# The order of score tiles and everything else inside a step of a three-unit attention pipeline

## Chip, cores and metric

One NeuronCore of a Trainium2 chip runs the kernel. The metric is the device time of one execution in microseconds (us), lower is better; the time before is the median of 3 runs.

## What is computed

The program embeds tokens, mixes them with one low-rank attention layer, routes each of 16 sequences to an expert, runs three 8-head attentions for each sequence, and ends with a feed-forward layer. The change is in the three attentions. In the reference they are (cut):

```
def _spatial_experts(xn, idx, in_w, in_b, out_w, out_b):      # "S", 512 x 512, 8 heads of 16
    att = softmax(einsum('bthd,bshd->bhts', q, k), axis=-1)
    o = einsum('bhts,bshd->bthd', att, v).reshape(B, T, D)
...
def _temporal_experts(...):                                    # "T", causal
    logits = where(causal, einsum('bthd,bshd->bhts', q, k) * HD ** (-0.5), -inf)
...
def _cross_mha(q_in, kv_in, ...):                              # "C", q from S's output, k and v from T's
...
fused = _cross_mha(spatial_out, temporal_out, ...)
```

## The kernel before, in words

`attend` works on 48 units: S, T and C of each of 16 sequences. A unit has 32 score tiles (8 heads by 4 blocks of 128 rows). Each unit goes through four stages, and a software pipeline has four units at work at once. Time is cut into slots of 32 steps (`TILES`). In a slot TensorE (called PE in the rows) works for:

- unit `kn`, the next: three projections to q, k and v, at steps 3, 9 and 12 to 15 (`PROJECT_AT`, L1200 and L1204)
- unit `ka`: one score tile a step (`score`, L1217, 128 rows by the keys). VectorE (DVE) reduces each tile to the row maxima, negated (`reduce`, L1022; for T with the causal mask, L1018)
- unit `kb`: one logit tile a step from step 8 on (`LAG`), transposed, with the maxima folded in as further rows of the contraction (`logits`, L1237). ScalarE (ACT) turns each into exponentials (L1122). From step 17 on every fourth step has a weighted sum (`weigh`, L1256, four matmuls side by side)
- unit `ko`, the oldest: its last 8 logit tiles at steps 0 to 7, its last weighted sums at steps 1, 5, 9 and 13, and its output matmul at steps 29 and 30 (`output`, L1273 and L1276)

The slots go round in three kinds, named here by the unit that is scored: an S slot, a T slot, a C slot. The middle of the program is a hardware loop over such triples. In a T slot the score tiles of the four row blocks have 128, 256, 384 and 512 keys in turn; the tile number modulo 4 tells the width. In an S or C slot all score tiles are 512 wide.

The maxima of a unit are turned (transposed, L1226) in two halves by `turn_maxima`: the first half at step 19 of the slot in which the unit is scored, the second at step 6 of the next slot. VectorE copies each turned half out (`ng`, L1032) after its reductions 18 and 5. VectorE also keeps the values `va` (L1043) after reduction 16, swaps the sums (`s_right`, L1059) after reduction 21 (`SWAP_AT`), and takes the output of `ko` (L1082 or L1089) after reduction 31. ScalarE makes the reciprocal `s_recip` (L1149) from the swapped sums at `RECIP_AT`, by which GpSimd (POOL) scales `oT`.

Two rings of three PSUM banks couple the engines: score tile n waits until VectorE has reduced tile n-3, and logit tile n until ScalarE has read tile n-3. One further bank, the desk, is shared by projections, turned maxima and outputs, strictly one after the other (`desk_free`, `desk_full`): so the turn at step 19 waits until `va` is kept, and the k projection at step 9 waits until the second half of the maxima (`ng`) is copied out. Each engine works strictly in the order in which `slot_program` writes its instructions; no scheduler moves them.

Of the kernel before, what the change touches and what calls it, by code (L numbers as in the profile page):

```python
# [37 lines left out]
WEIGH_AFTER = 9  # L38
VALUES_AT = 16
GROUP_1_AT, GROUP_2_AT = (30, 31), (14, 15)  # L40
SWAP_AT, RECIP_AT = 21, 23
OUTPUT_AT, KEEP_AT = 29, 31
PROJECT_PARTS, OUTPUT_PARTS = (1, 1, 4), 2
LAG = 8
# [20 lines left out]
def exists(b):  # L65
    return not isinstance(b, int) or 0 <= b < B
# [14 lines left out]
def desk_use(name, b):  # L81

    if name[0] in "qkv" and name[1] == "S" and isinstance(b, int) and b == 0:
        return "qkv".index(name[0])
    i = b - DESK_BATCH[name]
    order = [u for s in DESK for u in s]
    at = order.index(name)
    if isinstance(i, int):
        return desk_count(i) + sum(exists(i + DESK_BATCH[u]) for u in order[:at])
    return DESK_FIRST + DESK_USES * (i - STEADY[0]) + at  # L90


def unit_no(kind, b):

    if kind == "C":
        return 3 * B - 1 if isinstance(b, int) and b == B - 1 else 3 * b + 4
    if isinstance(b, int) and b == 0:
        return "ST".index(kind)
    return 3 * b - 1 + "ST".index(kind)


def ring_place(kind, b, n, ring):

    steady = {"S": -1, "T": 0, "C": 4}
    u = unit_no(kind, b) if isinstance(b, int) else steady[kind] % 3
    assert 3 * TILES % ring == 0
    return (TILES * u + n) % ring


def group_place(kind, b, q):  # L110

    return ring_place(kind, b, 4 * q, 4 * RP) // 4


def at_least(eng, sem, value):

    if not isinstance(value, int) or value > 0:
        eng.wait_ge(sem, value)
# [524 lines left out]
def attend(nc, shared, s_in, s_out, t_in, t_out, c_in, c_out, c_bias):  # L643
# [3 lines left out]
    with ExitStack() as ctx:  # L647
# [90 lines left out]
        def units(i, slot):  # L738

            return ((("T", i), ("S", i), ("C", i - 2), ("T", i - 1)),  # L740
                    (("C", i - 1), ("T", i), ("S", i), ("C", i - 2)),
                    (("S", i + 1), ("C", i - 1), ("T", i), ("S", i)))[slot]
# [19 lines left out]
        def first_key(kind, tile):  # L762

            return P * (tile // 4 % NB) if kind == "T" else 0
# [41 lines left out]
        with nc.Block() as block:  # L806
# [370 lines left out]
            def _(pe):  # L1177

                def project(kind, b, c, part):

                    if not exists(b):
                        return
                    source = {"S": xn, "T": xt, "C": t_outT if c else oT_S}[kind]
                    weight = w_fold if kind == "C" and c == 0 else w_in[kind]
                    use = desk_use("qkv"[c] + kind, b)
                    if part == 0:
                        at_least(pe, desk_free, use)
                        if kind == "C":
                            if c == 0:
                                pe.wait_ge(fold_in, 16 * b + 16)  # L1190
                                pe.wait_ge(o_ready, unit_no("S", b) + 1)
                            else:
                                pe.wait_ge(desk_free, desk_use("oT", b) + 1)
                        elif c == 0:
                            pe.wait_ge(win_in[kind], 16 * b + 16)
                            pe.wait_ge(affine_done, input_no({"S": "xn", "T": "xt"}[kind], b) + 1)
                    width = T // PROJECT_PARTS[c]
                    at = slice(width * part, width * part + width)
                    if c < 2:
                        last = nc.tensor.matmul(desk[:, at], weight[:, P * c:P * c + P], source[:, at],  # L1200
                                                start=True, stop=True)
                    else:
                        for n in range(width // P * part, width // P * (part + 1)):
                            last = nc.tensor.matmul(desk[:, P * n:P * n + P], source[:, P * n:P * n + P],  # L1204
                                                    w_in[kind][:, W_V:W_V + P], start=True, stop=True)
                    if part == PROJECT_PARTS[c] - 1:
                        last.then_inc(desk_full, 1)

                def score(kind, b, n):

                    u = unit_no(kind, b)
                    if n == 0:
                        pe.wait_ge(stack_in[kind], 16 * 2 * NPROD * (b + 1))
                    at_least(pe, reduced, TILES * u + n - RL + 1)
                    hd, tb = n // NB, n % NB
                    keys = P * (tb + 1) if kind == "T" else T
                    nc.tensor.matmul(psum[:, ring_place(kind, b, n, RL), 0:keys], qs[kind][0:RA, hd, P * tb:P * tb + P],  # L1217
                                     ks[kind][0:RA, hd, 0:keys], start=True, stop=True).then_inc(scored, 1)

                def turn_maxima(kind, b, half):  # L1220

                    if not exists(b):
                        return
                    pe.wait_ge(reduced, TILES * unit_no(kind, b) + HALF * (half + 1))
                    at_least(pe, desk_free, desk_use("hm"[half] + kind, b))
                    nc.tensor.transpose(desk[0:HALF, 0:P], mx[kind][:, HALF * half:HALF * half + HALF], ident[:])\  # L1226
                        .then_inc(desk_full, 1)
# [12 lines left out]
                def weigh(kind, b, q):  # L1240

                    u = unit_no(kind, b)
                    g, s = q // NB, q % NB
                    if kind == "T":
                        pe.wait_ge(cut, 2 * NB * b + q + 1)
                    else:
                        pe.wait_ge(exped, TILES * u + 4 * q + 4)
                    if q == 0:
                        pe.wait_ge(v_ready[kind], b + 1)
                        pe.wait_ge(desk_free, desk_use("v" + kind, b) + 1)  # L1250
                        at_least(pe, high_out, u)
                    if q == NB:
                        pe.wait_ge(low_out, u + 1)
                    t0 = first_key(kind, 4 * q)
                    for j in range(4):
                        last = nc.tensor.matmul(sums[32 * j:32 * j + 32, t0:T], va[kind][:, s, g, j, :],  # L1256
                                                probs[:, group_place(kind, b, q), j, t0:T], start=(s == 0),
                                                stop=(kind == "T" or s == NB - 1), skip_group_check=(kind == "T"))
                    last.then_inc(summed, 1)
# [21 lines left out]
                def slot_program(i, slot):  # L1281
                    (kn, bn), (ka, ba), (kb, bb), (ko, bo) = units(i, slot)
                    for n in range(TILES):
                        if exists(ba):
                            score(ka, ba, n)
                        if n == TURN_AT[0]:
                            turn_maxima(ka, ba, 0)
                        if n == TURN_AT[1]:
                            turn_maxima(kb, bb, 1)
                        for c in range(3):  # L1290
                            if 0 <= n - PROJECT_AT[c] < PROJECT_PARTS[c]:
                                project(kn, bn, c, n - PROJECT_AT[c])
                        if n < LAG and exists(bo):
                            logits(ko, bo, TILES - LAG + n)
                        if n >= LAG and exists(bb):
                            logits(kb, bb, n - LAG)
                        q, rest = divmod(n - LAG - WEIGH_AFTER, 4)
                        if rest == 0 and q < 0 and exists(bo):
                            weigh(ko, bo, q + 8)
                        if rest == 0 and q >= 0 and exists(bb):  # L1300
                            weigh(kb, bb, q)
                        if 0 <= n - OUTPUT_AT < OUTPUT_PARTS and exists(bo) and ko != "S":
                            output(ko, bo, n - OUTPUT_AT)

# [13 lines left out]
                last.then_inc(folded, 1)  # L1318
                pe.wait_ge(fold_kept, 2)
                whole_loop(pe, slot_program)  # L1320


# [246 lines left out]
```

## Time and profile before

| | before |
|---|---|
| median of 3 runs | 1693.22 us (1692.04 to 1693.26) |
| the profiled execution, its own time | 1697.35 us |
| its span in the trace | 1695.5 us |
| granted TensorE clock, mean | 0.938 of full speed; 1.00 in the slots shown |
| TensorE busy (matmul records) | 1521.0 us, 90% |
| VectorE busy | 1242.6 us, 73% |
| ScalarE busy | 1102.5 us, 65% |
| GpSimd busy | 1018.9 us, 60% |

All times of the trace are counted from the start of the span. A matmul's record lasts longer than the array is occupied by it, because matmuls overlap, so for TensorE the distance between the starts of two matmuls tells more than busy time. In the windows shown below the columns are the stretch and its length in us, then the busy us (and number of instructions) of PE, PEld (TensorE's weight loads), DVE, ACT and POOL, the granted clock as a share of 2.4 GHz, the DMA engines' share and GB/s. In the timelines they are the start in us, the duration in us, engine, line, operation, written<-read, shapes, and in brackets the idle time before the instruction with what ended it.

The share of busy time is a mean over the whole program; what follows reads single slots.

### The profile page before, as it was taken

The page shows a single profiled execution, that of the slowest core. Times are in us where ns is not written, and L with a number is a line of the kernel's source. Part 1 is how long each engine was busy: PE and PEld are TensorE (multiplying, and loading weights), DVE is VectorE, ACT ScalarE, POOL GpSimd, SP SyncE. Part 2 cuts the span into 40 slices and gives each one's busy share as a digit, 9 for nine tenths or more (in the row PEclk, how much of TensorE's full clock was granted, in tenths as well). Part 3 has the DMA queues.
Part 4 walks back from the last instruction along what each step waited for, and adds up shares of the span by engine and source line. Part 5 has one row for each costly group of instructions (what it writes and reads, how often), then busy time and mean ns, then how long its engine had stood idle before and what let it go on. Part 6 is the DMA issues. An engine that isn't in the chain of part 4 may idle for free. (4 is left out here: it accounts for less than half of the span.)

```text
span 1695.5 us, 37358 instructions
## 1 busy us (share of the span) xinstructions
PE 1521.0 (90%) x8662; PEld 660.5 (39%) x8662; DVE 1242.6 (73%) x3454; ACT 1102.5 (65%) x2137; POOL 1018.9 (60%) x1375
## 2 busy tenths in 40 slices
PE   2767975889999999999999999999999999875998
PEld 0215962233333333333333333333333333212665
DVE  4995866478787878878787887878788887353442
ACT  1432770647878777787877878787777878823333
POOL 6841435466685677767567677757767775423443
PEclk9767986879999999999999999999999999957999
DMA  1321117365454565456456546546645643020221
GB/s 41 77 54 31 45 32 108 50 81 72 70 83 67 70 75 84 62 74 81 61 75 77 77 60 83 75 60 81 77 72 65 85 63 55 10 30 29 62 67 56
DMA packets 134645, 109.27 MB, mean 64 GB/s; under 512 B 24128, under 2 KB 127552, under 8 KB 134592
## 3 DMA queue, kind: packets, MB, share of 16 engines
q1 hardware_dynamic: 132544, 104.45, 41.9%
q0 software_dynamic: 2048, 4.20, 1.0%
q8 instruction: 23, 0.38, 0.1%
q14 instruction: 30, 0.25, 0.1%
HBM read 19.26 MB, written 8.39 MB: 16 GB/s over the span
## 5 line engine op out<-in xcount | busy, mean ns | idle before, releaser
L1122 ACT ACTIVATE probs<-psum 128x512 f32<-128x512 f32 (+3 forms) x1536 | 757.9, 550 | 256.2 <-PE psum L1237 247.4
L1022 DVE TENSOR_REDUCE mx_S<-psum 128x1 f32<-128x512 f32 x512 | 324.7, 679 | 50.3 <-PE psum L1217 50.0
L1022 DVE TENSOR_REDUCE mx_C<-psum 128x1 f32<-128x512 f32 x512 | 316.3, 676 | 32.0 <-PE psum L1217 32.0
L1018 DVE CUSTOM_DVE_ANT_0 psum<-psum,causal 128x128 f32<-128x128 f32 (+3 forms) x512 | 241.4, 515 | 95.3 <-PE psum L1217 94.2
L1217 PE MATMUL psum<-ks_S,qs_S 96*128 96x512 bf16 x512 | 197.0, 395 | 17.9 <-DVE mx_S L1022 8.7
L1217 PE MATMUL psum<-ks_C,qs_C 96*128 96x512 bf16 x512 | 199.8, 398 | 12.2 <-DVE mx_C L1022 9.5
L1237 PE MATMUL psum<-qs_C,ks_C 99*128 99x512 bf16 x512 | 188.6, 387 | 3.3 <-ACT probs L1122 2.9
L1237 PE MATMUL psum<-qs_S,ks_S 99*128 99x512 bf16 x512 | 188.0, 384 | 0.2 <-ACT probs L1122 0.2
L903 POOL CAST parts_q<-f_q 128x512 bf16<-128x512 f32 x48 | 29.2, 609 | 251.1 <-ACT f_q L1113 250.6
L1217 PE MATMUL psum<-ks_T,qs_T 96*128 96x128 bf16 (+3 forms) x512 | 157.4, 310 | 5.1 <-DVE mx_T L1018 3.7
L1237 PE MATMUL psum<-qs_T,ks_T 99*128 99x256 bf16 (+3 forms) x512 | 152.3, 302 | 1.8 <-ACT probs L1122 1.7
L1256 PE MATMUL psum<-probs,va_C 128*32 128x512 f32 x1024 | 137.2, 608 | 0.8 <-ACT u_all L1142 0.6
L1256 PE MATMUL psum<-probs,va_S 128*32 128x512 f32 x1024 | 136.4, 604 | 1.7 <-ACT u_all L1142 0.5
L891 POOL TENSOR_SCALAR_AFFINE_SELECT probs<-probs 128x512 f32<-128x512 f32 x128 | 81.1, 634 | 57.4 <-ACT probs L1122 56.7
L1217 PEld LDWEIGHTS psum<-ks_C,qs_C 96*128 96x128 bf16 x512 | 49.9, 98 | 167.0 <-DVE mx_C L1022 121.2
L1217 PEld LDWEIGHTS psum<-ks_S,qs_S 96*128 96x128 bf16 x512 | 50.0, 98 | 154.5 <-DVE mx_S L1022 111.0
L1469 ACT ACTIVATE gT<-psum,b 128x512 f32<-128x512 f32 x64 | 44.0, 687 | 95.2 <-PE psum L1489 95.2
L1217 PEld LDWEIGHTS psum<-ks_T,qs_T 96*128 96x128 bf16 x512 | 50.6, 99 | 138.6 <-DVE mx_T L1018 95.5
L1256 PE MATMUL psum<-probs,va_T 128*32 128x512 f32 (+3 forms) x1024 | 96.0, 447 | 3.2 <-POOL probs L891 2.4
L957 POOL TENSOR_TENSOR s_all<-s_all,s_high 128x512 f32<-128x512 f32 x48 | 60.9, 1269 | 24.9 <-ACT u_high L1132 24.1
L317 POOL DMA_INDIRECT h<-in_table,ids x64 | 61.4, 960 | 21.4 <-issue 17.4
L1237 PEld LDWEIGHTS psum<-qs_C,ks_C 99*128 99x128 bf16 x512 | 49.5, 98 | 63.4 <-ACT probs L1122 27.5
(182 smaller groups left out, 2720.1 us busy)
## 6 DMA issues: line engine op xcount, KB each, us to landing
qs_S<-parts_q SPq DMA_DIRECT2D x96, 128.0 KB, 4.4
ks_S<-parts_k SPq DMA_DIRECT2D x96, 128.0 KB, 4.8
qs_T<-parts_q SPq DMA_DIRECT2D x96, 128.0 KB, 4.5
ks_T<-parts_k SPq DMA_DIRECT2D x96, 128.0 KB, 4.6
qs_C<-parts_q SPq DMA_DIRECT2D x96, 128.0 KB, 4.4
ks_C<-parts_k SPq DMA_DIRECT2D x96, 128.0 KB, 4.8
w_in_S<-in_s_in SPq DMA_DIRECT2D x16, 257.0 KB, 2.8
w_in_T<-in_t_in SPq DMA_DIRECT2D x16, 257.0 KB, 2.7
```

What stands on the lines that cost most here:

```text
L317: nc.gpsimd.indirect_dma_start(h[:, NB * b + n, :], None, table, bass.IndirectOffsetOnAxis(ap=ids[:, NB * b + n:NB * b + n + 1].bitcast(U3 ...
L891: nc.gpsimd.affine_select(out=diagonal, in_=diagonal, compare_op=ALU.is_ge, fill=0.0, base=0, pattern=[[0, 4], [1, P]], channel_multiplier ...
L903: nc.gpsimd.tensor_copy(parts[c][:, 0, :], f32[c][:]).then_inc(hi_done, 1)
L957: nc.gpsimd.tensor_tensor(s_all[:], s_all[:], s_high[:], ALU.add).then_inc(s_merged, 1)
L1018: nc.vector.tensor_tensor_reduce(tile[:, 0:last_key], tile[:, 0:last_key], causal[:, T - last_key:T], 1.0, NEG, ALU.add, ALU.max, mx[kind] ...
L1022: nc.vector.tensor_reduce(mx[kind][:, n:n + 1], tile, AX_X, ALU.max, negate=True).then_inc(reduced, 1)
L1122: nc.scalar.activation(probs[:, group_place(kind, b, n // 4), n % 4, t0:T], psum[:, LOGITS + ring_place(kind, b, n, RC), t0:T], ACT.Exp, s ...
L1217: nc.tensor.matmul(psum[:, ring_place(kind, b, n, RL), 0:keys], qs[kind][0:RA, hd, P * tb:P * tb + P], ks[kind][0:RA, hd, 0:keys], start=T ...
L1237: nc.tensor.matmul(psum[:, bank, t0:T], ks[kind][0:RB, hd, P * s:P * s + P], qs[kind][0:RB, hd, t0:T], start=True, stop=True).then_inc(log ...
L1256: last = nc.tensor.matmul(sums[32 * j:32 * j + 32, t0:T], va[kind][:, s, g, j, :], probs[:, group_place(kind, b, q), j, t0:T], start=(s == 0),
L1469: nc.scalar.activation(gT[:, odd, f, :], psum[:, 1 + f, :], ACT.Gelu, bias=b1[:, f:f + 1])\
```

## The change

In TensorE's `slot_program` the score tile of a step is written after the turns, projections, logit tile and weighted sums of that step, where it was written before them. The output matmul stays behind the score tile. On ScalarE the reciprocal moves from step 23 to step 24, one exponential later. VectorE's, GpSimd's and the DMA queue's programs are the same; no instruction is added or removed.

```
-SWAP_AT, RECIP_AT = 21, 23
+SWAP_AT, RECIP_AT = 21, 24
...
                 def slot_program(i, slot):
                     (kn, bn), (ka, ba), (kb, bb), (ko, bo) = units(i, slot)
                     for n in range(TILES):
-                        if exists(ba):
-                            score(ka, ba, n)
                         if n == TURN_AT[0]:
                             turn_maxima(ka, ba, 0)
...
                         if rest == 0 and q >= 0 and exists(bb):
                             weigh(kb, bb, q)
+                        if exists(ba):
+                            score(ka, ba, n)
                         if 0 <= n - OUTPUT_AT < OUTPUT_PARTS and exists(bo) and ko != "S":
                             output(ko, bo, n - OUTPUT_AT)
```

On TensorE, in the first T slot that also has projections (written out ahead of the loop), from step 3 to step 9, before the change:

```order
L1217 MATMUL psum<-ks_T,qs_T 128x512
L1200 MATMUL psum<-oT_S,w_fold 128x512
L1217 MATMUL psum<-ks_T,qs_T 128x128
L1217 MATMUL psum<-ks_T,qs_T 128x256
L1217 MATMUL psum<-ks_T,qs_T 128x384
L1226 MATMUL psum<-ident,mx_S 16x128
L1217 MATMUL psum<-ks_T,qs_T 128x512
L1217 MATMUL psum<-ks_T,qs_T 128x128
L1237 MATMUL psum<-qs_S,ks_S 128x512
L1217 MATMUL psum<-ks_T,qs_T 128x256
L1200 MATMUL psum<-t_outT,w_in_C 128x512
```

The same stretch after it:

```order
L1217 MATMUL psum<-ks_T,qs_T 128x384
L1200 MATMUL psum<-oT_S,w_fold 128x512
L1217 MATMUL psum<-ks_T,qs_T 128x512
L1217 MATMUL psum<-ks_T,qs_T 128x128
L1217 MATMUL psum<-ks_T,qs_T 128x256
L1226 MATMUL psum<-ident,mx_S 16x128
L1217 MATMUL psum<-ks_T,qs_T 128x384
L1217 MATMUL psum<-ks_T,qs_T 128x512
L1237 MATMUL psum<-qs_S,ks_S 128x512
L1217 MATMUL psum<-ks_T,qs_T 128x128
L1200 MATMUL psum<-t_outT,w_in_C 128x512
```

The kinds of matmul follow each other as before; in every place of a score tile stands the tile before it (384 keys where 512 stood, and so on). The turn of `mx_S` now follows tile 5 and not tile 6.

On TensorE, around the turn at step 19 of the same slot, before the change:

```order
L1256 MATMUL psum<-probs,va_S 32x512 x4
L1217 MATMUL psum<-ks_T,qs_T 128x384
L1237 MATMUL psum<-qs_S,ks_S 128x512
L1217 MATMUL psum<-ks_T,qs_T 128x512
L1226 MATMUL psum<-ident,mx_T 16x128
L1237 MATMUL psum<-qs_S,ks_S 128x512
```

And after it:

```order
L1256 MATMUL psum<-probs,va_S 32x512 x4
L1217 MATMUL psum<-ks_T,qs_T 128x256
L1237 MATMUL psum<-qs_S,ks_S 128x512
L1217 MATMUL psum<-ks_T,qs_T 128x384
L1226 MATMUL psum<-ident,mx_T 16x128
L1237 MATMUL psum<-qs_S,ks_S 128x512
```

The turn of the first half of T's maxima keeps its place among TensorE's instructions and stands behind tile 18 where it stood behind tile 19.

On ScalarE, in the second slot with a reciprocal, as one piece of the difference:

```order
 L1122 ACTIVATE probs<-psum 128x384
 L1122 ACTIVATE probs<-psum 128x256 x4
-L1122 ACTIVATE probs<-psum 128x128 x3
-L1149 ACTIVATE s_recip<-s_right 128x512
-L1122 ACTIVATE probs<-psum 128x128
+L1122 ACTIVATE probs<-psum 128x128 x4
+L1149 ACTIVATE s_recip<-s_right 128x512
 L1122 ACTIVATE probs<-psum 128x512 x4
```

One more exponential of 128 columns now stands ahead of the reciprocal.

## Rows read from the trace of the kernel before

**Rows 1.** The page's busy time by engine.

```profile
PE 1521.0 (90%) x8662; PEld 660.5 (39%) x8662; DVE 1242.6 (73%) x3454; ACT 1102.5 (65%) x2137; POOL 1018.9 (60%) x1375
```

**Rows 2.** Windows: an S, a T and a C slot (from VectorE's first reduction to the next).

```profile
711.43:736.88 25.45, 25.08 (x155) 9.72 (x154) 22.51 (x42) 19.78 (x41) 17.71 (x25) 1.00 0.54 81
736.88:762.08 25.20, 24.88 (x154) 9.72 (x150) 17.93 (x74) 21.26 (x41) 16.67 (x22) 1.00 0.55 69
762.08:786.25 24.17, 23.26 (x142) 8.73 (x134) 21.19 (x40) 17.66 (x39) 17.94 (x26) 1.00 0.55 71
```

**Rows 3.** Waits of the whole span: us in total, times, longest.

```profile
DVE ng L1032 <- PE psum L1226: 41.1, 48, 4.5
```

**Rows 4.** Timeline, TensorE, S slot, steps 6, 8 and 9.

```profile
715.41 0.39 PE L1217 MATMUL psum<-ks_S,qs_S 96*128 96x512 bf16 x1
...
716.31 0.38 PE L1237 MATMUL psum<-qs_C,ks_C 99*128 99x512 bf16 x1
717.02 0.39 PE L1217 MATMUL psum<-ks_S,qs_S 96*128 96x512 bf16 x1 [0.33 <-DVE mx_S L1022]
717.24 1.02 PE L1200 MATMUL psum<-xt,w_in_T 128*128 128x512 f32 x2
```

**Rows 5.** Timeline, VectorE, the same stretch.

```profile
716.08 0.28 DVE L1032 TENSOR_SCALAR ng<-psum 16x128 f32<-16x128 f32 x1 [0.39 <-PE psum L1226]
716.29 2.46 DVE L1022 TENSOR_REDUCE mx_S<-psum 128x1 f32<-128x512 f32 x4
```

**Rows 6.** Timeline, T slot: VectorE's copy, and TensorE at steps 8 and 9.

```profile
741.32 0.28 DVE L1032 TENSOR_SCALAR ng<-psum 16x128 f32<-16x128 f32 x1 [1.07 <-PE psum L1226]
...
741.71 0.38 PE L1237 MATMUL psum<-qs_S,ks_S 99*128 99x512 bf16 x1
742.29 0.28 PE L1217 MATMUL psum<-ks_T,qs_T 96*128 96x256 bf16 x1 [0.20 <-DVE mx_T L1018]
```

**Rows 7.** Timeline, TensorE, C slot, steps 8 and 9.

```profile
767.61 0.38 PE L1237 MATMUL psum<-qs_T,ks_T 99*128 99x512 bf16 x1
767.97 0.39 PE L1217 MATMUL psum<-ks_C,qs_C 96*128 96x512 bf16 x1
```

**Rows 8.** Timeline, S slot: swap on VectorE; TensorE's score tiles 22, 25 and 26.

```profile
728.05 0.70 DVE L1059 STREAM_SHUFFLE s_right<-s_all 128x512 f32<-128x512 f32 x1
...
727.88 0.39 PE L1217 MATMUL psum<-ks_S,qs_S 96*128 96x512 bf16 x1
...
728.99 0.38 PE L1237 MATMUL psum<-qs_C,ks_C 99*128 99x512 bf16 x1
729.41 0.39 PE L1217 MATMUL psum<-ks_S,qs_S 96*128 96x512 bf16 x1
...
730.94 0.39 PE L1217 MATMUL psum<-ks_S,qs_S 96*128 96x512 bf16 x1
```

**Rows 9.** Timeline, TensorE, T slot, steps 24 to 25 and 28 to 29.

```profile
754.43 0.38 PE L1237 MATMUL psum<-qs_S,ks_S 99*128 99x512 bf16 x1
754.85 0.28 PE L1217 MATMUL psum<-ks_T,qs_T 96*128 96x256 bf16 x1
...
757.16 0.38 PE L1237 MATMUL psum<-qs_S,ks_S 99*128 99x512 bf16 x1
757.48 0.28 PE L1217 MATMUL psum<-ks_T,qs_T 96*128 96x256 bf16 x1
```

**Rows 10.** Timeline, S slot: values kept on VectorE, and the turn at step 19.

```profile
723.99 0.75 DVE L1043 TENSOR_TENSOR va_T<-psum,w_in_T 128x256 f32<-128x256 f32 x2
...
725.59 0.27 PE L1226 MATMUL psum<-ident,mx_S 128*16 128x128 f32 x1
```

**Rows 11.** Timeline, C slot: its second half on VectorE, ScalarE and TensorE.

```profile
780.28 6.04 DVE L1022 TENSOR_REDUCE mx_C<-psum 128x1 f32<-128x512 f32 x10
...
780.49 0.63 ACT L1149 ACTIVATE s_recip<-s_right 128x512 f32<-128x512 f32 x1 [0.78 <-DVE s_right L1059]
...
781.00 0.39 PE L1217 MATMUL psum<-ks_C,qs_C 96*128 96x512 bf16 x1 [0.62 <-DVE mx_C L1022]
```

More of the change, by code:

```diff
@@ L40 @@
 GROUP_1_AT, GROUP_2_AT = (30, 31), (14, 15)
-SWAP_AT, RECIP_AT = 21, 23
+SWAP_AT, RECIP_AT = 21, 24
 OUTPUT_AT, KEEP_AT = 29, 31
@@ L1283, in slot_program @@
                     for n in range(TILES):
-                        if exists(ba):
-                            score(ka, ba, n)
                         if n == TURN_AT[0]:
@@ L1301, in slot_program @@
                             weigh(kb, bb, q)
+                        if exists(ba):
+                            score(ka, ba, n)
                         if 0 <= n - OUTPUT_AT < OUTPUT_PARTS and exists(bo) and ko != "S":
```

## The prediction

> **What bounds the kernel now.** I read the page first. TensorE has the most busy time, then VectorE, ScalarE and GpSimd [rows 1]. But matmul records overlap, so this settles nothing. The windows come next, cut at VectorE's first reduction of each slot: an S, a T and a C slot take 25.45, 25.20 and 24.17 us, together 74.8 us at full clock, and VectorE is busy for 22.5, 17.9 and 21.2 us of them [rows 2]. The hardware loop runs 13 such triples (`STEADY`), and partly filled ones stand ahead of it and behind it.
>
> What decides is the distance between the starts of TensorE's matmuls. A matmul with 512 columns is followed 0.22 us later by the next one where nothing is late (717.02 to 717.24) [rows 4]. Where a distance is larger, TensorE stood still for the difference. Laid over a whole triple, TensorE streams almost without a break in the S and T slots and in the first half of a C slot, and stands still at few places:
>
> - S slot, score tile 9: it comes 0.71 us after the logit tile before it (716.31 to 717.02), so 0.49 us are lost [rows 4].
> - T slot, tile 9: 0.58 us, 0.36 lost [rows 6]. C slot, tile 9: 0.36 us, 0.14 lost [rows 7].
> - S slot, tile 25: 0.42 us, 0.20 lost [rows 8]. T slot, tile 25: 0.42, 0.20 lost; tile 29: 0.32, 0.10 lost [rows 9].
> - second half of the C slot: here VectorE is the bound. It does ten reductions in 6.04 us without a gap, one each 0.60 us, and tile 25 waits for it (idle 0.62 us by the record's modelled end) [rows 11].
>
> Two causes stand behind the first five. Tile 9 waits for reduction 6, and reduction 6 waits behind the copy `ng`, which waits for the turn at step 6. That turn stands behind score tile 6, which stands behind the weighted sum of step 5. VectorE has reduced tile 5 long before: it idles 0.39 us ahead of `ng` in the S slot [rows 5] and 1.07 us in the T slot [rows 6], 41.1 us in 48 waits in all [rows 3]. And tile 25 waits for reduction 22, which stands behind the swap (0.70 us) [rows 8].
>
> **The change part by part.** No instruction is added or removed, so all durations stay. On TensorE the sequence of kinds is the same; only the score tile in each place is the one before. I call place n what held tile n. Place n now holds tile n-1. Seen from TensorE, then, every reduction comes in the same place, and the extras of VectorE (`ng`, `va`, swap, outputs) come one reduction later. The ring of three is unchanged in these terms: place n waits for the reduction of place n-3.
>
> *The copy `ng` at step 5.* It now follows the reduction of place 6, so reduction and turn run side by side. S slot: the tile in place 6 starts at 715.41 and takes 0.39 [rows 4], so its reduction can begin at 715.84 and ends near 716.5 with the 0.67 us of one (2.46 less three spacings of 0.60) [rows 5]; before it began at 716.29. Place 9 can follow at about 716.55, when TensorE is free anyway (716.31 + 0.22 = 716.53). The 0.49 us are gone. T slot and C slot have 0.36 and 0.14 to lose and VectorE was idle longer there (1.07 us in the T slot), so these go too. Sum 0.99 us for each triple. What is late next: the k projection in place 9 waits for `ng` to free the desk. `ng` now starts after the reduction, near 716.45, and takes 0.28 us: 716.7, while TensorE reaches the projection at 716.55 + 0.22 = 716.77. The margin is under 0.1 us. If it is missed in each slot by as much as 0.1 us, 48 slots give back 4.8 us.
>
> *The swap.* It comes after the reduction of place 22, so place 25 no longer waits for it: 0.20 + 0.20 us back, and 0.10 at tile 29 of the T slot, whose reduction of place 26 is now of the 256-key tile and shorter. Sum 0.50 us for each triple. The 0.70 us of the swap used to lie under the weighted sum of step 21; now they lie behind it, so I follow them [rows 8]. The tile in place 22 starts at 727.88 and is done at 728.27, its reduction ends near 728.97, so place 25 can go at 729.2, as soon as TensorE is free (728.99 + 0.22). The swap lasts to about 729.6, the next reduction (place 23) to 730.2. Place 26 waits for that one; it comes 1.53 us after place 25 (729.41 to 730.94), now at 730.7. So the swap is hidden again, with 0.5 us to spare. Bounds: all 0.50 us back, or none; I take all.
>
> *The values `va`.* One reduction later, 0.60 us. They end at 724.74 in the S slot and the turn at step 19, which waits for them on the desk, starts at 725.59 [rows 10]: 0.85 us of cover, 0.25 left. No cost. VectorE's wait for the turn gets no longer, since the turn stands one tile earlier.
>
> *Projections, outputs and weighted sums* keep their places. The output at step 29 now stands behind the next score tile, which feeds VectorE 0.4 us earlier after the long block; VectorE is not the bound there. No gain is counted.
>
> *The reciprocal.* The swap ends one reduction later, 0.60 us, and the reciprocal one exponential later. In the C slot ScalarE already waits 0.78 us for it [rows 11] and has slack (17.7 busy of 24.2 us) [rows 2]. In the T slot ScalarE is busy for 21.3 of 25.2 us, so a longer wait could be absorbed. Counted at nothing; if the wait were 0.3 us longer in each of the 32 fuller slots and reached TensorE, it would cost 10 us, which is in the upper end of the range.
>
> *The C slot's second half* stays as long as it is, since VectorE's work there is the same.
>
> *The sum.* 0.99 + 0.50 = 1.49 us for a triple, 13 triples in the loop: 19.4 us. The partly filled triples at both ends have smaller waits of the same kind, about 1 us together. Against this, VectorE runs one tile behind TensorE, which costs 0.6 us once. 19.8 us off. The profiled execution took 1697.35 us by its own clock, 4.1 us above the median of the runs; its own would become 1677.6, and the median 1693.2 - 19.8 = 1673.4 us. I forecast 1674.
>
> **A rule of the skill against this.** Rows first: weight loads are busy for 39% of the span, VectorE for 73% [rows 1]. The Trainium skill, "Perfetto Trace Analysis", section "Identifying the Most-Contended Engine", judges TensorE's headroom by its weight loads and not by its matmul records; by it VectorE would be the engine to relieve here. What that would make of the time is the fourth rival below. The starts of the matmuls 0.22 us apart [rows 4] speak against it: the array is taken, although weight loads are not.
>
> **The rivals.**
> - *Half of it (chance 0.17).* The `ng` part works, the swap part does not: the swap's 0.70 us stop place 26 instead of place 25. Gain 0.99 x 13 = 13 us, 1680 us; with the desk missed by 0.1 us each time, 1685. For it: the swap loses its cover under a weighted sum. Against: VectorE has 3 to 7 us of idle time in the S and T slots [rows 2].
> - *The waits only move, or ScalarE hands the gain back (0.07).* 1690 to 1696 us. For it: several engines are each two thirds to nine tenths busy. Against: the places of loss are fed by VectorE alone.
> - *Slower (0.05).* The turn at step 19 catches VectorE before `va` is kept, and TensorE stands. The cover is 0.85 us, one reduction takes 0.60 of it [rows 5, 10]. Each 0.1 us that the values come later than I think, beyond 0.25 us, costs 4.8 us over 48 slots; the gain is eaten up at 0.41 us of stall a slot, and at 0.55 us the time is 1700 us.
> - *VectorE is the bound everywhere (0.04).* Then what counts is its idle time ahead of `ng`, 41.1 us [rows 3]: 1652 us. Against: in the T slot it is busy for 17.9 of 25.2 us [rows 2], and cannot be the bound there.
>
> **How the numbers follow.** My forecast's own case has 0.67, with 1670 to 1679 us. The range of 1667 to 1687 adds the half case whole and a few us below for waits in the first and last slots; it leaves out the second, third and fourth rival, 0.16, and a little of the tails. A change of 0.2%, 3.4 us, is about what can be told from none. Faster: 0.67 + 0.17 + 0.04 and a part of the second rival, 0.89; same 0.06; slower 0.05.
>
> **What would show it.** Right: the wait of `ng` for the turn falls from 41 us to under 5; in S, T and C slots tiles in place 9 and 25 follow 0.22 us after the logit tile (0.1 after a narrow one); an S slot takes about 24.8 us, a T slot 24.6, a C slot 24.0, a triple 73.3; TensorE still idles in the second half of the C slot. Wrong: a new wait on TensorE ahead of L1226 or of L1200 for the desk, a wait of L1149 above 24 us in the T and S slots that ends in late logit tiles, or a longer C slot.

## The result, and the profile after

The changed kernel takes **1672.98 us** (median of 4 runs, 1671.79 to 1673.13), against 1693.24 for the kernel before (1692.04 to 1693.40, 4 runs on the same chip). The ratio is 0.9882 (95% interval 0.9871 to 0.9894), so 20.3 us less. The forecast was 1674 us, its sum 19.8 us less.

The page's busy line and the windows of an S, a T and a C slot, cut at VectorE's first reduction as in [rows 2] (columns: PE, PEld, DVE, ACT, POOL busy, granted clock, DMA share, GB/s):

```profile
PE 1517.6 (91%) x8662; PEld 661.0 (40%) x8662; DVE 1245.2 (75%) x3454; ACT 1106.5 (66%) x2137; POOL 1020.2 (61%) x1375
```

```profile
702.17:726.91 24.74, 24.74 (x154) 9.57 (x146) 22.52 (x41) 19.71 (x40) 17.14 (x24) 1.00 0.54 76
726.91:751.40 24.49, 24.40 (x154) 9.66 (x150) 18.00 (x74) 21.19 (x40) 16.64 (x22) 1.00 0.56 71
751.40:775.59 24.19, 23.89 (x146) 9.00 (x142) 21.21 (x41) 18.08 (x40) 18.57 (x27) 1.00 0.57 76
```

No engine executes fewer instructions (the counts are those of [rows 1]). The S slot is 0.71 us shorter, the T slot 0.71, the C slot not at all (24.17 before): a triple falls from 74.82 to 73.42 us, by 1.40. I forecast 1.49. Over the 39 slots that the hardware loop accounts for (score tile 0 of the sixth slot to that of the 45th), the trace shows 971.96 us before and 954.31 now: 17.65 us. The first five slots lose 0.46 us, the last four gain 1.46 (up to their last score tile) and what follows them 1.27. These ends say little: the kernel of e2 below takes the same 971.9 us as before over the 39 slots, and differs by 1.3 us in the first five. The two spans differ by 24.4 us, and 4.5 us of that lie ahead of the first score tile, where nothing was changed; the profiled execution of before stood 4.1 us above its median.

Now the places. TensorE, S slot, steps 8 and 9, and VectorE in the same stretch:

```profile
706.52 0.38 PE L1237 MATMUL psum<-qs_C,ks_C 99*128 99x512 bf16 x1
706.80 0.39 PE L1217 MATMUL psum<-ks_S,qs_S 96*128 96x512 bf16 x1
707.03 1.08 PE L1200 MATMUL psum<-xt,w_in_T 128*128 128x512 f32 x2
```

```profile
706.05 0.69 DVE L1022 TENSOR_REDUCE mx_S<-psum 128x1 f32<-128x512 f32 x1 [0.15 <-PE psum L1217]
706.66 0.27 DVE L1032 TENSOR_SCALAR ng<-psum 16x128 f32<-16x128 f32 x1
```

The tile in place 9 comes 0.28 us after the logit tile, where it took 0.71 [rows 4]. `ng` starts right behind a reduction, with no idle time ahead of it (0.39 us in [rows 5]). But it ends only at 706.93, and the projection waits for the desk until then. TensorE's weight loads of place 9 and of the projection, before and after:

```profile
717.01 0.10 PEld L1217 LDWEIGHTS psum<-ks_S,qs_S 96*128 96x128 bf16 x1 [0.82 <-DVE mx_S L1022]
717.11 0.33 PEld L1200 LDWEIGHTS psum<-xt,w_in_T 128*128 128x128 f32 x2
```

```profile
706.80 0.10 PEld L1217 LDWEIGHTS psum<-ks_S,qs_S 96*128 96x128 bf16 x1 [0.40 <-DVE mx_S L1022]
706.98 0.30 PEld L1200 LDWEIGHTS psum<-xt,w_in_T 128*128 128x128 f32 x2
```

The projection's weights now start 0.18 us after those of the score tile, just behind the end of `ng`, where it was 0.10. The logit tile after the projection comes 0.92 us after the projection's start (707.95), where it was 0.87 (718.11 less 717.24). So the desk was missed by some 0.06 us in each S slot.

The same on TensorE in the T slot (place 9 at 731.69) and in the C slot (756.71):

```profile
731.47 0.38 PE L1237 MATMUL psum<-qs_S,ks_S 99*128 99x512 bf16 x1
731.69 0.22 PE L1217 MATMUL psum<-ks_T,qs_T 96*128 96x128 bf16 x1
731.75 1.08 PE L1200 MATMUL psum<-t_outT,w_in_C 128*128 128x512 f32 x2
732.66 0.38 PE L1237 MATMUL psum<-qs_S,ks_S 99*128 99x512 bf16 x1
...
756.50 0.38 PE L1237 MATMUL psum<-qs_T,ks_T 99*128 99x512 bf16 x1
756.71 0.38 PE L1217 MATMUL psum<-ks_C,qs_C 96*128 96x512 bf16 x1
```

0.22 and 0.21 us, where it was 0.58 and 0.36 [rows 6, 7]. In the T slot the logit tile behind the projection now comes 0.97 us after place 9 (732.66 less 731.69); before it came 1.16 us after it (743.45 less 742.29). The tile in place 9 has 128 keys and not 256, which explains 0.06 of these 0.19 us (a logit tile follows the one in 0.06 us and the other in 0.12); the other 0.13 were not forecast.

The swap and place 25 in the S slot (VectorE, then TensorE):

```profile
718.78 0.72 DVE L1059 STREAM_SHUFFLE s_right<-s_all 128x512 f32<-128x512 f32 x1
```

```profile
718.83 0.38 PE L1237 MATMUL psum<-qs_C,ks_C 99*128 99x512 bf16 x1
719.05 0.38 PE L1217 MATMUL psum<-ks_S,qs_S 96*128 96x512 bf16 x1
```

Place 25 (719.05) follows in 0.22 us while the swap still runs; before it took 0.42 [rows 8]. Three places on, place 28 follows its logit tile by 0.26 us (721.68 to 721.94): the reductions behind the swap are 0.05 us late there.

The output matmul at step 29 stood behind the weighted sum, and now stands behind the score tile. T slot, before and after:

```profile
758.91 0.71 PE L1273 MATMUL psum<-w_out_C,oT 128*128 128x128 f32 x4
759.46 0.33 PE L1217 MATMUL psum<-ks_T,qs_T 96*128 96x384 bf16 x1
```

```profile
748.12 0.61 PE L1273 MATMUL psum<-w_out_C,oT 128*128 128x128 f32 x4
748.56 0.38 PE L1237 MATMUL psum<-qs_S,ks_S 99*128 99x512 bf16 x1
```

What follows it starts after 0.44 us instead of 0.55; in the S slot after 0.44 instead of 0.54 (723.70 to 724.14; before, 733.78 to 734.32). These 0.11 and 0.10 us come in every S and T slot of the loop, some 2.7 us in all, and the forecast counted no gain there.

Last, the end of a T slot, where not all is gone: TensorE at steps 28 and 29, and ScalarE ahead of them.

```profile
746.46 0.22 PE L1217 MATMUL psum<-ks_T,qs_T 96*128 96x128 bf16 x1
746.68 0.39 PE L1237 MATMUL psum<-qs_S,ks_S 99*128 99x512 bf16 x1
```

```profile
744.53 0.63 ACT L1149 ACTIVATE s_recip<-s_right 128x512 f32<-128x512 f32 x1 [0.16 <-DVE s_right L1059]
745.07 3.02 ACT L1122 ACTIVATE probs<-psum 128x512 f32<-128x512 f32 x6
```

Place 29 (746.46) is 0.22 us behind the logit tile at 746.24 (0.32 in [rows 9]). But the next logit tile comes 0.22 us later, where one behind a tile of 128 keys takes 0.06. It waits for an exponential. The reciprocal started 0.16 us late for want of the swap, and six exponentials then run without a gap. This is a loss that the prediction counted at nothing. The whole wait of the reciprocal for the swap grew from 24.0 us (19 times) to 32.1 (37 times), a sign of being wrong that the prediction had named; that of `ng` for the turn fell from 41.1 us to 7.0, in 3 waits, where under 5 was forecast.

### The profile page after: what moved, and what is told of

It reads as the page before. It is cut to its first block and busy times, and to the rows that moved or that the text cites. A ratio compares the mean times of both kernels' runs of the same rounds, so it can differ in the third digit from the quotient of the medians.

```text
span 1671.1 us, 37358 instructions
## 1 busy us (share of the span) xinstructions
PE 1517.6 (91%) x8662; PEld 661.0 (40%) x8662; DVE 1245.2 (75%) x3454; ACT 1106.5 (66%) x2137; POOL 1020.2 (61%) x1375
```

## The experiments

The runs were made on several chips, whose kernel before stood between 1693.1 and 1697.5 us; ratios are to the before of the same chip. "Triple" is the distance of score tiles 0 of two S slots in the trace (74.81 before, 73.41 after the change).

**1 and 2. The order without the reciprocal's step, and that step alone.**

```diff
# e1: the changed kernel
-SWAP_AT, RECIP_AT = 21, 24
+SWAP_AT, RECIP_AT = 21, 23
# e2: the kernel before
-SWAP_AT, RECIP_AT = 21, 23
+SWAP_AT, RECIP_AT = 21, 24
```

> The changed order on TensorE alone, the reciprocal left at step 23. My theory (VectorE's extras one reduction later are what counts): ScalarE now reaches the reciprocal up to 0.5 us before the swap is done in the S and T slots, but the late exponential reaches TensorE only after three more logit tiles, so 1673 to 1676 us. Rival (the reciprocal's step carries a real part of the gain, since ScalarE is 80% busy): 1680 us or more, with TensorE waiting for ScalarE at logit tiles 18 and 19.

> The reciprocal at step 24 alone, the old order on TensorE. My theory: nothing, within 1 us of 1693. Rival (ScalarE's wait for the swap cost time before): 2 us or more faster.

e1: 1680.77 us, ratio 0.9925 (0.9912 to 0.9939). e2: 1693.12, ratio 1.0000 (0.9991 to 1.0009). The number that changes nothing in the old order is worth 7.8 us in the new one (7.4 over the 39 slots of the trace). The T slot of e1 on ScalarE and TensorE:

```profile
744.98 0.63 ACT L1149 ACTIVATE s_recip<-s_right 128x512 f32<-128x512 f32 x1 [0.63 <-DVE s_right L1059]
```

```profile
745.74 0.28 PE L1217 MATMUL psum<-ks_T,qs_T 96*128 96x256 bf16 x1
746.15 0.39 PE L1237 MATMUL psum<-qs_S,ks_S 99*128 99x512 bf16 x1
```

The reciprocal waits 0.63 us at the head of ScalarE's queue, the exponentials behind it are late, and a logit tile starts 0.41 us after a score tile of 256 keys instead of 0.12. e1's T slot takes 24.86 us against 24.38; its triple is 73.98. My theory of no effect fell.

**3 and 4. The two parts of the gain, each alone in the kernel before.**

```diff
# e3
-TURN_AT, KEEP_MAXIMA_AT = (19, 6), (18, 5)
+TURN_AT, KEEP_MAXIMA_AT = (19, 6), (18, 6)
# e4
-SWAP_AT, RECIP_AT = 21, 23
+SWAP_AT, RECIP_AT = 22, 24
```

> The old order on TensorE; VectorE copies the second half of the maxima out after reduction 6 and not 5. My theory: this alone takes away the wait of tile 9, 0.99 us of each triple, 13 us: 1680 us (1678 to 1682). In S, T and C slots tile 9 follows 0.22 us after its logit tile, while tile 25 still comes 0.42 us after its own. Rival (it is the place of the score tile that matters, not the copy's): no change, 1693.

> The old order on TensorE; the swap after reduction 22 and the reciprocal at step 24. My theory: takes away the waits of tile 25 (0.20 us in the S and in the T slot), perhaps tile 29 (0.10 us in the T slot), 5 to 6.6 us: 1687 to 1688 us. Rival (the swap loses its cover under the weighted sum and stops tile 26): 1693 or slower.

e3: 1680.17 us, ratio 0.9927 (0.9913 to 0.9940), 13 us less, the number that was worked out (13 x 0.99). But in the trace its 39 slots are only 10.9 us shorter, 0.84 us a triple: the S slot is 0.38 us shorter (the desk is missed here too), the T slot 0.36 and the C slot 0.15. The other 2 us lie ahead of these slots and behind them. e4: 1689.67, ratio 0.9981 (0.9972 to 0.9990): 3.5 us less where 5 to 6.6 were expected, and 1.6 over the 39 slots. In the S slot it gives the 0.19 us. In the T slot it gives nothing; e4, VectorE's swap and TensorE around it:

```profile
748.63 0.75 DVE L1059 STREAM_SHUFFLE s_right<-s_all 128x512 f32<-128x512 f32 x1
```

```profile
746.54 1.06 PE L1256 MATMUL psum<-probs,va_S 128*32 128x512 f32 x8
...
748.43 0.38 PE L1237 MATMUL psum<-qs_S,ks_S 99*128 99x512 bf16 x1
748.75 0.28 PE L1217 MATMUL psum<-ks_T,qs_T 96*128 96x256 bf16 x1
...
751.01 0.22 PE L1217 MATMUL psum<-ks_T,qs_T 96*128 96x128 bf16 x1
751.16 0.39 PE L1237 MATMUL psum<-qs_S,ks_S 99*128 99x512 bf16 x1
```

The swap starts 2.09 us after the weighted sum of step 21 (748.63 less 746.54), because the tile reduced ahead of it has 384 keys. In the changed kernel that place holds the 256-key tile (TensorE, then VectorE):

```profile
741.76 1.06 PE L1256 MATMUL psum<-probs,va_S 128*32 128x512 f32 x8
```

```profile
743.65 0.75 DVE L1059 STREAM_SHUFFLE s_right<-s_all 128x512 f32<-128x512 f32 x1
```

There the swap starts 1.89 us after the same weighted sum. So in e4 tile 25 keeps 0.10 us of its wait (0.32 from 748.43), and logit tiles at the slot's end are late for ScalarE (0.15 instead of 0.06 at 751.16).

**5 and 6. Only the extras, or all but the extras.** e5 gives the kernel before VectorE's extras one reduction later in the old order; e6 takes the changed kernel and moves them one reduction earlier, so that they stand as they did.

```diff
# e5: the kernel before
-TURN_AT, KEEP_MAXIMA_AT = (19, 6), (18, 5)
+TURN_AT, KEEP_MAXIMA_AT = (19, 6), (19, 6)
-VALUES_AT = 16
+VALUES_AT = 17
-SWAP_AT, RECIP_AT = 21, 23
+SWAP_AT, RECIP_AT = 22, 24
# e6: the changed kernel
-TURN_AT, KEEP_MAXIMA_AT = (19, 6), (18, 5)
+TURN_AT, KEEP_MAXIMA_AT = (19, 6), (17, 4)
-VALUES_AT = 16
+VALUES_AT = 15
-SWAP_AT, RECIP_AT = 21, 24
+SWAP_AT, RECIP_AT = 20, 23
```

> The old order on TensorE, but all of VectorE's extras inside a slot one reduction later: values after 17, maxima after 19 and 6, swap after 22, reciprocal at step 24. My theory says that the change is this shift seen from the other side, so the time is that of the changed kernel, 1673 us within 1.5 us. Rival (the narrower T tile behind each weighted sum, or the output behind one more score tile, gives part of the gain): 1676 us or slower.

> The changed order on TensorE with VectorE's extras one reduction earlier: values after 15, maxima after 17 and 4, swap after 20, reciprocal at step 23. My theory: the extras stand to TensorE's work as before the change, so the gain is gone: 1693 us within 2 us, and the copy of the second half of the maxima waits some 40 us in all again. Rival (the order on TensorE gains by itself): clearly under 1690 us.

e5: 1683.18 us, ratio 0.9922 (0.9909 to 0.9936). e6: 1687.76, ratio 0.9947 (0.9934 to 0.9961). Both missed. "The same as one reduction later" is untrue of the T slot (24.79 us against 24.38), whose tiles have 128 to 512 keys, and of the S slot by the output's place (24.53 against 24.43: the 0.10 us above). The C slot takes 24.47 us, less than in the changed kernel (24.60); 12 below tells why. And e6 keeps about 8 us, 7.0 of them over the 39 slots: its T slot takes 24.59 us where it took 25.09 and its S slot 24.92 instead of 25.10, although `ng`, `va` and swap stand as before. The output's place, which e6 shares with the changed kernel, is 2.7 us of it. In the S slot the wait of place 9 is back:

```profile
713.75 0.38 PE L1237 MATMUL psum<-qs_C,ks_C 99*128 99x512 bf16 x1
714.46 0.39 PE L1217 MATMUL psum<-ks_S,qs_S 96*128 96x512 bf16 x1 [0.33 <-DVE mx_S L1022]
```

**8. The widths alone.** The changed kernel, with the T unit's tiles taken as 256, 384, 512, 128 keys, so that each place has the width that it had before:

```diff
-hd, tb = n // NB, n % NB
+hd, tb = n // NB, (n + 1) % NB if kind == "T" else n % NB
# and VectorE's reduction takes the same width and writes the column of that tile (cut)
```

> The changed kernel, with T's score tiles taken in the order 256, 384, 512, 128 keys within each head, so that each place in TensorE's order has the width that it had before the change (the tile behind each weighted sum is again the 384 wide one). Theory now, from the two kernels with VectorE's extras shifted: they missed some 7 us because reduction 22, and with it swap, reciprocal and exponentials, comes later behind a wider tile in the T slot. So this takes back most of that: about 0.5 us of each triple, 1678 to 1681 us where the changed kernel has 1673, with TensorE waiting at tile 25 and at the logit tiles of steps 28 and 29 of the T slot. Rival (the widths do not matter, it is the place of output and turn): 1673 within 1.5 us.

1677.78 us, ratio 0.9908 (0.9892 to 0.9925), against 0.9882: 4.4 us of the gain are gone. The T slot takes 24.70 us instead of 24.38; the 0.10 us at the swap and the late logit tiles of e4 are back in it, some 0.19 us together. The other 0.13 are lost at the projection behind place 9, which holds a tile of 256 keys again (at 732.99; this kernel's line numbers are two higher):

```profile
733.20 1.12 PE L1202 MATMUL psum<-t_outT,w_in_C 128*128 128x512 f32 x2
734.15 0.38 PE L1239 MATMUL psum<-qs_S,ks_S 99*128 99x512 bf16 x1
```

The logit tile comes 1.16 us after place 9, as before the change, and not 0.97. So the widths are a term of their own, at two places: what meets the swap, and what stands ahead of the projection. What makes the second slow isn't shown.

**7. The values one step later.**

```diff
-VALUES_AT = 16
+VALUES_AT = 17
```

> The changed kernel with the values kept after reduction 17 and not 16. It measures the slower rival: the turn at step 19 waits for the values on the desk. In the changed kernel's trace the values are done about 0.2 to 0.3 us before the turn in S and T slots. One reduction later they stop it by about 1.1 us in the S slot and 1.0 us in the T slot; the C slot, where VectorE is the bound, loses nothing. 13 triples and the partly filled ones: 27 to 31 us slower, 1700 to 1704 us. Rival (TensorE's stall is hidden by VectorE's own work): 1673 to 1680 us.

1724.14 us, ratio 1.0165 (1.0151 to 1.0178): 28 us slower than before, 48 slower than the change, where 27 to 31 were expected. S slot, TensorE, and VectorE's values:

```profile
733.91 0.38 PE L1217 MATMUL psum<-ks_S,qs_S 96*128 96x512 bf16 x1
735.30 0.28 PE L1226 MATMUL psum<-ident,mx_S 128*16 128x128 f32 x1 [1.01 <-DVE va_T L1043]
```

```profile
734.50 0.74 DVE L1043 TENSOR_TENSOR va_T<-psum,w_in_T 128x256 f32<-128x256 f32 x2
```

The turn starts 1.39 us after the score tile instead of 0.22. This prices the rival *slower*, and the price of one step is more than one reduction (0.60 us): the values now follow the reduction of a tile that stands behind the weighted sum of step 17, so they start 14.6 us after score tile 0 of the slot instead of 13.3. The C slot, where I had expected slack, loses 0.9 us as well (25.54).

**9, 10 and 12. Where the C slot's 0.14 us went.** In the changed kernel (TensorE, end of a C slot and start of the next S slot):

```profile
773.92 0.39 PE L1217 MATMUL psum<-ks_C,qs_C 96*128 96x512 bf16 x1
774.40 0.28 PE L1237 MATMUL psum<-qs_T,ks_T 99*128 99x256 bf16 x1
774.65 0.39 PE L1217 MATMUL psum<-ks_S,qs_S 96*128 96x512 bf16 x1
```

The first logit tile takes 0.48 us instead of 0.22. e9 moved the wait for the transfer of the stack from score tile 0 to the slot's head. e10 did that too, and moved the C slot's projection of the values into its second half.

```diff
# e9, in score(); and the same wait at the head of the slot
-if n == 0:
-    pe.wait_ge(stack_in[kind], 16 * 2 * NPROD * (b + 1))
# e10, beside it
+at = LATE_V if c == 2 and slot == 2 else PROJECT_AT[c]
-if n == VALUES_AT:
+if n == (LATE_V + 4 if slot == 2 else VALUES_AT):
# and the order of the users of the desk to match (cut)
```

> The changed kernel, with TensorE's wait for the stacked operands of a unit (an instruction of its own ahead of its first score tile) moved to the start of the slot. Theory: in the C to S passage the first score tile starts 0.13 us after the reduction that it waits for, where others start 0.07 us after it; that extra wait instruction stands in the way, and it ate the gain of tile 9 in the C slot. 0.06 to 0.14 us for each triple, 1 to 2 us faster than the changed kernel. Rival: no difference.

> The kernel of the early stack wait, and in the C slot alone the v projection at steps 22 to 25 instead of 12 to 15 with the values kept after reduction 26, the turn ahead of them on the desk. Theory: in the first half of a C slot TensorE is the bound and VectorE in the second, where TensorE idles some 0.9 us; moving 0.9 us of TensorE's work over gives 0.4 to 0.5 us for each triple, 6 us: 1666 to 1668 us. Rival (a new wait: desk or VectorE starved behind the weighted sum of step 25): 1672 us or slower.

e9: 1672.60 us, ratio 0.9882 (0.9866 to 0.9899), no difference: that theory fell. e10: 1675.21, ratio 0.9895 (0.9878 to 0.9911), no faster: the work that was moved away had been cover. With it gone the weighted sum of step 17 waits for ScalarE (e10, TensorE), and the C slot takes 24.76 us instead of 24.59:

```profile
763.21 0.28 PE L1236 MATMUL psum<-qs_T,ks_T 99*128 99x256 bf16 x1
763.79 1.06 PE L1255 MATMUL psum<-probs,va_T 128*32 128x512 f32 x8 [0.29 <-ACT u_high L1133]
```

What stands ahead of the late logit tile are the records of TensorE's sequencer at the hardware loop's end (line 798): an ALU_OP at 773.91, a COMPARE_BRANCH of 215 ns at 774.01, register work from 774.28. Before the change the same records (784.81) lay beside the wait of score tile 0 for VectorE. e12 closes the loop elsewhere, between steps 25 and 26 of the C slot; it has the reciprocal of e11, below, as well.

```diff
-def slot_program(i, slot):
+def slot_program(i, slot, first, end):
-    for n in range(TILES):
+    for n in range(first, end):
-whole_loop(pe, slot_program)
+whole_loop_from(pe, slot_program, 2, 26)
```

> The changed kernel with the reciprocal at step 25, and TensorE's hardware loop closed between step 25 and step 26 of the C slot instead of at the end of the C slot (the instructions and their order are the same). Compare with e11, 1669.25 us against a before of 1693.51, ratio 0.9859. Theory (the loop's back edge on TensorE's sequencer costs the time ahead of the first logit tile of the S slot): there VectorE is the bound in the C slot's second half, so the edge is hidden. The interval ahead of the first logit tile of the S slot falls from 487 to about 220 ns, score tile 0 starts no later after the end of the reduction that it waits for than the other tiles, 0.06 to 0.27 us for each of 13 turns, 0.8 to 3.5 us in all: ratio 0.984 to 0.9855, 1666 to 1668.5 us. Rival 1 (the first logit tile only moves forward and then waits longer for VectorE, which has its own work to catch up with): ratio 0.9859 within 0.0005. Rival 2 (the edge shows wherever it stands, since TensorE's queue is fed too late after it): the interval at step 26 of the C slot grows by 0.25 us and the ratio stays or gets worse, 1669 to 1672 us.

1674.30 us, ratio 0.9865 (0.9849 to 0.9882) to a before of 1697.46. TensorE at step 26 of the C slot and at the new S slot (whose first logit tile is that at 777.60, behind the score tile at 777.37):

```profile
773.78 0.39 PE L1217 MATMUL psum<-ks_C,qs_C 96*128 96x512 bf16 x1
774.26 0.39 PE L1237 MATMUL psum<-qs_T,ks_T 99*128 99x512 bf16 x1
...
777.60 0.27 PE L1237 MATMUL psum<-qs_T,ks_T 99*128 99x256 bf16 x1
777.97 0.39 PE L1217 MATMUL psum<-ks_S,qs_S 96*128 96x512 bf16 x1
```

The 0.48 us have moved to step 26, and the first logit tile follows in 0.23: the loop's end is what cost the time there. Its price is small: the triple falls from 73.22 (e11) to 73.12 us, since score tile 0 now waits for VectorE instead (0.37 us from 777.60). The C slot takes 24.47 us there, against 24.59 in e11; e3 and e5, in whose order the loop's end still lies beside the wait of score tile 0, have the same 24.47. 13 times 0.10 us can't be told in the whole time, and its ratio is not below e11's.

**11. The reciprocal one more step back.**

```diff
-SWAP_AT, RECIP_AT = 21, 24
+SWAP_AT, RECIP_AT = 21, 25
```

> The changed kernel with the reciprocal one more step back, at 25. Leaving it at 23 cost 7.8 us. Theory: that was because ScalarE stood at the reciprocal until the swap was done, and at 24 it no longer stands in S and T slots, so another step gives nothing: within 1 us of the changed kernel. Rival (the later the better): 2 us or more faster, and GpSimd's product the later.

1669.25 us (1668.47 to 1669.95), ratio 0.9859 (0.9843 to 0.9876). On the same chip e9, which times as the changed kernel does, took 1672.60 (1670.71 to 1673.52): 3.4 us less, where I had expected nothing (2.0 over the 39 slots). e11, TensorE at the end of the T slot, and ScalarE:

```profile
745.86 0.22 PE L1217 MATMUL psum<-ks_T,qs_T 96*128 96x128 bf16 x1
745.92 0.38 PE L1237 MATMUL psum<-qs_S,ks_S 99*128 99x512 bf16 x1
```

```profile
744.16 0.64 ACT L1149 ACTIVATE s_recip<-s_right 128x512 f32<-128x512 f32 x1
```

The reciprocal waits no more, the logit tile follows in 0.06 us, and the T slot takes 24.20 us instead of 24.38. This kernel is faster than the one before and than the changed one.

## Why the prediction was right, and where a term was off

The parts for one triple of the loop, from the distances between starts that are given above (the loop's end from the C slots, 24.60 us against 24.47 in e3, e5 and e12):

| part | forecast, us | measured, us |
|---|---|---|
| waits of place 9 (S, T, C) | 0.99 | 0.43 + 0.36 + 0.15 = 0.94 |
| waits of places 25 and 29 | 0.50 | 0.50 |
| desk missed in the S slot | 0 | -0.06 |
| place 28 of the S slot | 0 | -0.05 |
| late logit tile in the T slot | 0 | -0.16 |
| end of TensorE's loop | 0 | -0.13 |
| output behind the score tile (S, T) | 0 | 0.21 |
| projection of place 9 in the T slot | 0 | 0.13 |
| sum | 1.49 | 1.38 (the windows: 1.40) |

**`ng`, 0.99 us a triple: right in cause, a little too large.** All waits of place 9 are gone but for 0.06 us in the S slot. The margin at the desk, "under 0.1 us", did not hold there; it costs another 0.06. That e3 comes out at 13.0 us in the whole time is partly luck, since its slots give 10.9.

**The swap, 0.50 us a triple: right in size, short in cause.** The waits of places 25 and 29 are gone. But I had moved the swap by "one reduction" and used the tile's width only for place 29. e4, e5 and e8 show that the T slot's share is had only in part with the old widths, because the tile ahead of the swap has 256 keys now instead of 384. And the swap is not wholly hidden: 0.05 us show at place 28 of the S slot.

**The reciprocal, counted at nothing: mis-sized.** I weighed a wait of ScalarE against its idle share of the T slot (21.3 of 25.2 us busy [rows 2]). What decides is the run of exponentials behind it. At step 23 the new order loses 7.8 us (e1, inside my bound of 10); at step 24, 3.4 us are still left to be had (e11). That it is needed at all follows only from the swap coming later (e2).

**The C slot, 0.14 us: not gained (24.0 forecast, 24.19 measured).** The wait of place 9 is gone, but the second half is VectorE's, and score tile 0 of the next slot now stands behind a logit tile that the end of TensorE's loop makes 0.26 us late. Cut at score tile 0, a C slot took 24.63 us before and takes 24.60 now, but 24.47 in e3, e5 and e12, where the loop's end is covered: there the 0.14 us are had.

**The output, counted at nothing: overlooked.** I asked only what its new place does to VectorE, and not what it does to the output itself, which had cost 0.10 us more behind a weighted sum. Why it did isn't shown.

**The values and the turn at step 19: right,** with 0.07 us of wait in the C slot (the turn comes 0.29 us after its score tile), which the rest of that slot makes up for. e7 shows what the rival *slower* would have looked like one step on.

**The sum.** The loop gave 17.65 us where 19.4 were forecast; its two ends gave 2.3 where 0.4 were. Inside the loop the losses that I had at nothing (0.40 us a triple) nearly cancel with gains that I had at nothing (0.34). So the mechanism, waits behind `ng` and behind the swap, is right, and that the forecast lies within 0.5 us of the 20.3 measured is luck. The rivals *half of it* and *the waits only move* are out. *VectorE is the bound everywhere* is out as well: its work is the same and the time stopped at 1673, not 1652. The Trainium skill, "Perfetto Trace Analysis", section "Identifying the Most-Contended Engine", would still name VectorE here by its measure of weight loads, 75% against 40% (its other measure, matmul operations against the peak, is in no view here); the S slot's row with TensorE busy for 24.74 of 24.74 us, and its starts 0.22 us apart, say otherwise.

What stays open: where the gain outside the 39 slots comes from (1.9 to 2.6 us of the whole time in the change, e3 and e4, none in e2); and how the rest of e6's 8 us, behind the 2.7 of the output, divides between the widths and the shorter way from a score tile to the slot's end.

## What to carry to other kernels

In an in-order kernel whose engine streams, read the distances between starts, and ask of each gap which instruction the awaited one is queued behind; moving one by a step can free both. If tiles differ in width, a shift of the order by one is not a shift of the numbers by one: work it out for each kind of tile. Moving an instruction also changes what it stands behind: compare its own distance to the next start too, as with the output here. And when one engine's instruction moves back, look at the next engine's instruction that waits for it at the head of its queue, and move that back until it finds its input there.

## What was not expected of the hardware

- The end of the hardware loop costs TensorE 0.26 us at the first logit tile behind it (0.48 us instead of 0.22), with a COMPARE_BRANCH record of 215 ns. It moved with the loop's end in e12. The Trainium skill, "Advanced Engine Details and Errata", section "Control Flow Timing", states some 108 ns for a compare-and-branch; this trace shows twice that on every turn but the last, whose record lasts 83 ns.
- When the values that the turn waits for slip by one step past a weighted sum of eight matmuls, TensorE loses 1.1 us a slot (a triple of 76.66 us against 73.41), more than the 0.6 us of the reduction (e7).
- An output matmul takes 0.10 us more of TensorE's time behind a weighted sum than behind a score tile (0.54 and 0.55 us to the next start, against 0.44).
